# The two half-width rope combinations of a decoder layer, moved from VectorE to GpSimd

## The reference, cut to what matters

```
x = layernorm(x + self_attention(x))
x = layernorm(x + cross_attention(x, ctx))
h = x + attention(rope(rms_norm(x, norm1_w)), Wq, Wk, Wv, Wo)
h = h + moe(rms_norm(h, norm2_w))
out = layernorm(x + h)

rms_norm(x, w): x / sqrt(mean(x*x) + eps) * w
rope(x):  xe, xo = x[..., 0::2], x[..., 1::2]
          concat([xe*cos - xo*sin,  xe*sin + xo*cos])
```

## Time and profile before

| | us |
|---|---|
| median of 3 runs | 283.98 (283.62 to 284.4) |
| profiled execution | 283.89 |
| its span | 282.1 |
| busy: PE / DVE / ACT / POOL | 219.0 / 193.5 / 119.1 / 109.7 |
| the chain that ended last: PE / DVE / POOL | 62% / 16% / 6% |

### The profile page before, as it was taken

How to read it: one execution, slowest core, us unless ns; L and a number is a source line. 1 busy time by engine, 2 the same in 40 slices (tenths; PEclk the granted TensorE clock), 3 DMA queues, 4 the chain that set the end, 5 groups by cost and what they waited for, 6 DMA issues and landing times.

```text
span 282.1 us, 6021 instructions
## 1 busy us (share of the span) xinstructions
PE 219.0 (78%) x1736; PEld 195.2 (69%) x1737; DVE 193.5 (69%) x526; ACT 119.1 (42%) x393; POOL 109.7 (39%) x188
## 2 busy tenths in 40 slices
PE   0489999999999999997999752299999999940000
PEld 0368999899899887886998552188999999930000
DVE  7034799887799999997776348736767676733434
ACT  1436666567566654446654202043434434410000
POOL 0242235444555455442322240353553422017771
PEclk9999999999999999799999655579999999985555
DMA  7799700000008000000000000011211233011112
GB/s 239 171 364 344 167 3 0 2 0 3 2 3 224 0 2 3 1 0 12 9 13 19 19 12 0 20 29 31 70 51 47 44 48 39 19 37 47 55 47 74
DMA packets 21335, 16.00 MB, mean 57 GB/s; under 512 B 3033, under 2 KB 18465, under 8 KB 21313
## 3 DMA queue, kind: packets, MB, share of 16 engines
q1 hardware_dynamic: 19248, 12.02, 14.7%
q0 software_dynamic: 1344, 2.76, 4.8%
q10 hardware_dynamic: 720, 0.95, 1.0%
HBM read 11.78 MB, written 3.93 MB: 56 GB/s over the span
## 4 chain that ended last, share of the span: by engine, by line
PE 62%; DVE 16%; POOL 6%; issue 6%; DMA 4%; ACT 2%; SPq 2%; POOLq 0%; DVEq 0%; ACTq 0%
PE bank L665 12%; PE bank L559 11%; PE bank L481 9%; PE bank L676 7%; PE bank L533 7%; POOL yg L470 4%; DVE smax L872 3%; PE bank L569 3%; PE bank L529 3%; PE bank L576 2%; PE bank L517 2%; DVE x L924 2%; DMA bias_col<-in_L_xattn_bv 2%; PE bank L518 1%; PE bank L519 1%
## 5 line engine op out<-in xcount | busy, mean ns | idle before, releaser
L559 PE MATMUL bank<-vbd,pt_sb 128*128 128x34 f32 x384 | 46.3, 276 | 0.2 <-ACT pt_sb L755 0.2
L559 PEld LDWEIGHTS bank<-vbd,pt_sb 128*128 128x128 f32 x384 | 44.8, 192 | 0.3 <-ACT pt_sb L755 0.3
L458 POOL DMA_INDIRECT early<-xm_scratch,tok_i x26 | 25.8, 994 | 45.3 <-DMA early<-xm_scratch,tok_i 27.8
L872 DVE TENSOR_REDUCE smax<-bank 128x8 f32<-128x512 f32 x48 | 32.6, 679 | 13.3 <-PE bank L533 13.3
L665 PE MATMUL bank<-xgt,w_now 128*128 128x128 f32 x320 | 40.4, 281 | 0.4 <-ACT xgt L827 0.4
L665 PEld LDWEIGHTS bank<-xgt,w_now 128*128 128x128 f32 x320 | 38.7, 198 | 0.8 <-ACT xgt L827 0.8
L380 POOL TENSOR_TENSOR k<-kt,cst 128x512 f32<-128x512 f32 x24 | 25.2, 1052 | 33.1 <-ACT kt L745 33.1
L880 DVE TENSOR_TENSOR s_sb<-bank,smax 128x512 f32<-128x512 f32 x48 | 33.2, 691 | 2.1 <-PE bank L481 0.3
L831 ACT ACTIVATE s_sb<-bank,w_now 128x128 f32<-128x128 f32 x80 | 22.8, 368 | 23.8 <-PE bank L665 23.8
L533 PE MATMUL bank<-k,q 64*128 64x256 f32 x192 | 28.8, 411 | 0.0
L1092 DVE SCALAR_TENSOR_TENSOR pt_sb<-bank,w_now,s_sb 128x128 f32<-128x128 f32 x80 | 22.5, 343 | 7.3 <-ACT s_sb L831 6.6
(11 more groups left out here) (159 smaller groups left out, 345.4 us busy)
## 6 DMA issues: line engine op xcount, KB each, us to landing
w_up<-in_L_ffn_W SPq DMA_DIRECT2D x2, 2048.0 KB, 12.3
w<-in_L_ffn_W SPq DMA_DIRECT2D x8, 256.0 KB, 6.3
y_scratch<-eo SPq DMA_DIRECT2D x1, 1536.0 KB, 6.9
y_scratch<-eo SPq DMA_DIRECT2D x10, 128.0 KB
cst<-in_consts ACTq DMA_DIRECT2D x1, 672.5 KB, 4.0
early<-in_x SPq DMA_DIRECT2D x1, 512.0 KB, 5.9
early<-in_ctx SPq DMA_DIRECT2D x1, 512.0 KB, 4.2
xm_scratch<-xm SPq DMA_DIRECT2D x8, 64.0 KB, 1.5
```

The source lines that it names most:

```text
L458: pool.indirect_dma_start(xg[:, j, :], None, xm_d[:, :], bass.IndirectOffsetOnAxis(ap=tok_i[:, j:j + 1], axis=0)).then_inc(g_gather, 16)
L559: k = mm(ps_o[:, c:c + 34], pt_sb[:, h, (2 * b + jj) * P:(2 * b + jj + 1) * P], vbd[:, i, b, j, :, :].rearrange("k p c -> k (p c)"), start ...
L872: v.tensor_reduce(smax[:, b, :], ps_score[b][:, :].rearrange("q (p k) -> q p k", k=S), AX.X, ALU.max).then_inc(d_mx, 1)
```

## The change

The two combinations leave VectorE's `finish` and stand in a new GpSimd function, `rotate(it-3)`, called behind `expand_keys(it+2)`. They count up a counter of GpSimd (`g_xr`) in place of VectorE's (`d_xr`); TensorE's `turn_x` and VectorE's next `rope_a` wait on that. GpSimd waits on `d_ra` (both rope products written) before it combines them.

```diff
+            def rotate(n):
+
+                t = n - NT
+                if 0 <= t < NT:
+                    pool.wait_ge(d_ra, 2 * (t + 1))
+                    ra = rope_a[:, :].rearrange("q (h e) -> q h e", e=2)
+                    rbb = rope_b[:, :].rearrange("q (h e) -> q h e", e=2)
+                    half = D // 2
+                    g.tensor_tensor(xr[:, t, 0:half], ra[:, :, 0], rbb[:, :, 1], ALU.subtract).then_inc(g_xr, 1)
+                    g.tensor_tensor(xr[:, t, half:D], rbb[:, :, 0], ra[:, :, 1], ALU.add).then_inc(g_xr, 1)
...
                 if it + 2 < STEPS:
                     expand_keys(it + 2)
+                rotate(it - 3)
                 if it >= 4:
                     add_bias(it - 4)
...
-                    pe.wait_ge(d_xr, 2 * (t + 1))
+                    pe.wait_ge(g_xr, 2 * (t + 1))
...
                     if t >= 1:
-                        dve.wait_ge(d_xr, 2 * t)
+                        dve.wait_ge(g_xr, 2 * t)
                     for r, w in ((rope_a, rope_c), (rope_b, rope_s)):
                         v.scalar_tensor_tensor(r[:, :], x2[:, t, :], rstd[:, i, 3:4], w[:, :],
                                                ALU.mult, ALU.mult).then_inc(d_ra, 1)
-                    dve.wait_ge(d_ra, 2 * (t + 1))
-                    ra = rope_a[:, :].rearrange("q (h e) -> q h e", e=2)
-                    rbb = rope_b[:, :].rearrange("q (h e) -> q h e", e=2)
-                    half = D // 2
-                    v.tensor_tensor(xr[:, t, 0:half], ra[:, :, 0], rbb[:, :, 1], ALU.subtract).then_inc(d_xr, 1)
-                    v.tensor_tensor(xr[:, t, half:D], rbb[:, :, 0], ra[:, :, 1], ALU.add).then_inc(d_xr, 1)
```

More of the change, by code:

```diff
@@ L226, in decoder_kernel @@
         d_ra = sem("d_ra")
-        d_xr = sem("d_xr")
+        g_xr = sem("g_xr")
         d_xm = sem("d_xm")
```

## The result

| | before | after |
|---|---|---|
| median us (4 runs each) | 283.99 (283.62 to 284.4) | 280.35 (280.07 to 280.77) |
| profiled execution / its span | 283.89 / 282.1 | 280.07 / 278.3 |
| VectorE period in the rope stretch | 6.28 | 5.89 |
| ratio | | 0.9877, 95% interval 0.9858 to 0.9896 |

The change takes 3.6 us off; 280.7 was predicted. On another chip the same kernel gave 0.9875 (0.9851 to 0.9898).

A forecast was written before the change was run, and what follows sets the result against it. VectorE was taken to bound the kernel's rope stretch; 3.0 us (8 tiles x 0.38) plus 0.2 at the first tile made 3.2 off 283.89, so 280.7 us. The range was 279.4 to 282.4.

The forecast's parts named there:

- What bounds: Rope stretch: VectorE is full and sets the 6.28 us period; TensorE's own at full clock is 5.55.
- Removed work and wait: VectorE, each of 8 tiles: reciprocal starts 0.38 us earlier without two instructions and a wait, 3.0 us in all.
- The low end: VectorE, 8 tiles: only 0.27 us each if the pipe is emptied all the same, 2.2 us.
- First tile: `rope_b` there takes 0.34 us in place of 0.54, as GpSimd's bias add moves behind the combinations: 0.2 us more.
- A cover of 1.03 us: GpSimd: idle time left between the pair (0.66 us) and the next `row_scale`, so the pair costs nothing.
- the margin: First tile, GpSimd: pair, bias add and cast end at 83.98, `row_scale` is due at 84.11; a margin of 0.1.
- The hand-over: Stretch's end, VectorE's residual add releasing TensorE through ScalarE: VectorE still last by 0.3 us, low clock included.
- VectorE blocked by the pair: Rope turns: GpSimd's pair holds back the output scaling, 1.3 us slower less 0.2, 285.0; chance 0.04.
- Cover gone: GpSimd before `row_scale`: pair takes 2.06 us against 1.69 covered, no change at 283.7; chance 0.05.
- TensorE taking over: Late in the rope stretch: TensorE's clock falls once its lead is used up, costs 1.4 us, 282.1; chance 0.12.
- The clock behind the stretch: Around the routing: TensorE's low clock level may not move with the earlier work; 282.4 (0.07) or 279.5 (0.06).
- a late rise or fall: TensorE's clock around the routing: late rise costs 1.7 us, 282.4 (0.07); late fall returns 1.2, 279.5 (0.06).

The follow-up runs named there:

- keys_xr: Kernel before, with GpSimd's key expansion waiting for VectorE's two combinations: stretch 45.94 us, period 5.61, ratio to before 0.9822.
- keys_last: Changed kernel with GpSimd's pair of combinations ahead of its key expansion: stretch 44.82 us, ratio to the kernel before 0.9729.
- dve_late: Kernel before, both combinations still on VectorE but behind the next iteration's reciprocal: stretch 49.12 us, period 6.00, ratio 0.9963.
- bias_first: Changed kernel with the pair behind the bias add and cast at the first tile: stretch 48.25 us, ratio to the kernel before 0.9889.
- half: Kernel before with only the subtraction moved to GpSimd, addition and its wait kept on VectorE: stretch 50.22 us, period 6.16, ratio 0.9994.
- extra6: Changed kernel plus six unused 128x64 operations on GpSimd behind each pair: stretch 53.00 us, period 6.50, ratio to the kernel before 1.0069.
- keys_last_before: Kernel before plus a wait on `rope_b` in front of GpSimd's key expansion: stretch 52.78 us, period 6.47, ratio 1.0094.

## Why the prediction was right

**What bounds.** VectorE did: every edit of its list moved the period by what it took from the list, to within 0.03 us, with TensorE's clock up or down. It sets the stretch down to 5.6 us (`keys_xr`); below, TensorE's 5.44 to 5.56 does (`keys_last`).

**Removed work and wait.** 8 x 0.38 = 3.0 was the term; 6.28 - 5.89 = 0.39 a turn was measured. The low end, that a wait gives nothing back, is excluded by the 0.26 us from `rope_b` to the reciprocal, and by `dve_late`.

**First tile.** 0.2 forecast, 0.21 by `bias_first`. Together 3.2 forecast for the stretch, 3.33 measured.

**GpSimd.** 0.35 us for 128x64 from a line through two larger sizes; the rows show 0.35. A cover of 1.03 us forecast behind the pair, 1.04 found. At the first tile the margin was mis-sized, 0.1 for 0.40: the cast was taken at 0.45 and takes 0.28, and it overlaps with its neighbours. The trace of the kernel before had it already, at 0.34:

```profile
82.33 0.34 POOL L371 CAST b_lo<-b_raw 8x128 bf16<-8x128 f32 x1
```

**The hand-over.** Called the narrowest place, with 0.3 us of reserve; TensorE was idle there for 1.06. The sum had kept the low step of the clock in mid-stretch, and it did not come in the two profiled executions of the changed kernel. Whether the change keeps it away is open: `half` had one (0.89 and 0.84 in two neighbouring periods of 6.16), `dve_late` none in the stretch. `half` also bears out the way in which the sum counted: counted from the reciprocal of iteration 11, TensorE was ready 0.85 us earlier than before, where the five tiles before the last release make 5 x 0.12 + 0.2 = 0.80, VectorE's residual add came 1.15 earlier, and the idle time fell from 1.45 to 1.14. What would be left of it in the changed kernel with such a step was not measured.

**Rivals.** VectorE blocked by the pair: excluded by its rows after and by `extra6`. Cover gone: it exists, beyond 1.69 us. TensorE taking over did not happen. The clock behind the stretch moved with the kernel: by windows of 0.5 us it was low from 156.7 to 187.4 before and from 152.9 to 183.6 after, 30.7 us both times, so neither of the two prices of a late rise or fall was due.

**Slips.** The rows start up to 0.09 us off the end of the one before, not 0.08, and two thirds of 1.7 are 1.1, not 1.2. Neither matters to the sum.

**Not forecast.** 3.80 - 3.33 = 0.47 us of the span, for which the sum has no term, above all 0.50 in the experts. TensorE's clock came back 3.9 us after `xs` in place of 4.2, which is part of it; the changed kernel alone took 66.47 and 68.31 us for the same part in its two profiled executions, so it is not put down to the change.

## What to carry to other kernels

On an engine that is full, read start to start and not durations: two instructions of 0.23 and 0.22 us were worth 0.39 together with the wait in front of them, and 0.28 could be had with both left on the engine, by placing an independent instruction in between. When an instruction takes three times its usual length, look for the other engine's instruction beside it and ask what it will lie beside after it has been moved; a collision that is only shifted comes back at the next instruction that can collide. Here it went away once the other engine's instruction lay beside none of those, either because it waited for `rope_b` and the combinations had left the engine (`keys_last`), or because it waited for the combinations too (`keys_xr`).

## What the runs showed of the hardware

On VectorE, `rope_a`, `rope_b` and the addition, which read two tiles from the core's memory, were held by a GpSimd instruction that had started before them, and ended 0.07 to 0.15 us behind it (0.35 to 1.02, 0.34 to 0.54, 0.22 to 1.07 us). So was the normalisation (0.34 to 1.01), which reads one tile from there and two columns. The subtraction of `keys_last_before`, which started at 88.56, 0.04 us ahead of the expansion, kept its 0.23. Reciprocal, scaling and residual add, with an input from the accumulators, lay beside 1.05 us of GpSimd's work (`keys_xr`) and beside 2.3 us (`extra6`) without a difference, in `extra6` also the statistics, with one input, and the row maximum, which reads the accumulators. The Trainium skill, "SBUF — State Buffer", section "Who interferes with whom", tells it as a lock between the two engines, taken by VectorE for a second input or in its two-port mode. The instructions with two inputs agree with it, held in `keys_last_before` and free in `keys_xr`; that the normalisation ran in the two-port mode no run shows.

GpSimd's 128x64 operation took 0.35 us with interleaved inputs; six with contiguous ones ran 0.275 apart, the pair 0.31.
